# Cross-attention with layer norm on one core: the rounded copy of x moves from ScalarE to GpSimd, from the third 512 rows on

## What is computed

```python
qh = split_heads(q @ Wq.T + bq)            # q = x, (4, 2048, 512)
kh = split_heads(k @ Wk.T + bk)            # k = v = ctx, (4, 77, 512)
vh = split_heads(v @ Wv.T + bv)
scores = einsum('bhqd,bhkd->bhqk', qh, kh) / sqrt(32)
scores = where(mask == 0, -1e9, scores)
e = exp(scores - max(scores)) * mask
probs = e / (sum(e) + 1e-9)
attn = einsum('bhqk,bhkd->bhqd', probs, vh)
x = attn @ Wo.T + bo + residual            # residual = q
out = (x - mean(x)) / sqrt(var(x) + 1e-5) * ln_g + ln_b
```

## Time and profile before

| what | us |
| --- | --- |
| three runs, median | 617.98 |
| three runs, lowest to highest | 617.49 to 618.96 |
| the profiled execution, its device time | 615.88 |
| the profiled execution, its span | 614.1 |

### The profile page before, as it was taken

The page is one execution under the profiler, slowest core; times in us unless marked ns, Lnnn a source line. Parts: engine busy times, 40 slices in busy tenths (PEclk is TensorE's granted clock), DMA queues, the critical chain, the costliest instruction groups (busy, mean ns, idle before and its releaser), DMA issues.

```text
span 614.1 us, 15264 instructions
## 1 busy us (share of the span) xinstructions
PE 564.5 (92%) x5460; PEld 456.9 (74%) x5460; DVE 525.6 (86%) x801; ACT 504.6 (82%) x2288; POOL 437.5 (71%) x399
## 2 busy tenths in 40 slices
PE   2699398999999999999999999999999999999795
PEld 2588376777878788777877788777878788776574
DVE  4577558789998979898998989898998899899877
ACT  4449669899898989998898989998898999889521
POOL 2704443867588795789778886689678967786787
PEclk9989789999999999999999999999999999999899
DMA  8922730120045310640324412340424312202132
GB/s 310 318 88 57 225 88 1 52 99 3 11 140 188 138 53 10 216 147 3 94 93 155 155 64 75 122 148 3 126 76 141 153 51 104 105 2 99 76 138 102
DMA packets 36198, 64.91 MB, mean 106 GB/s; under 512 B 12443, under 2 KB 14491, under 8 KB 34075
## 3 DMA queue, kind: packets, MB, share of 16 engines
q1 hardware_dynamic: 35979, 63.94, 30.6%
q10 hardware_dynamic: 144, 0.00, 0.0%
HBM read 44.15 MB, written 19.46 MB: 104 GB/s over the span
## 4 chain that ended last, share of the span: by engine, by line
PE 84%; DVE 6%; SPq 5%; DMA 3%; issue 2%; POOL 0%; ACT 0%; DVEq 0%
PE qo_bank L420 54%; PE s_bank L420 17%; PE av_bank L508 11%; DVE E L803 2%; DMA Kd<-TP 2%; PE av_bank L420 1%; DMA Vp<-V_scratch 1%; DVE TP L832 1%; SPq L251 1%; SPq L330 1%; SPq L256 1%; DVE qo_bank L849 1%; DVE bn L855 1%; SPq L304 0%; DVE AT_lo L841 0%
## 5 line engine op out<-in xcount | busy, mean ns | idle before, releaser
L625 ACT ACTIVATE E<-E,neg_max 128x77 f32<-128x77 f32 x1024 | 352.2, 352 | 19.7 <-DVE neg_max L811 19.6
L625 ACT ACTIVATION_READ_ACCUMULATOR E<-E,neg_max 128x1 f32 x1024 | 196.8, 192 | 0.0
L1125 POOL TENSOR_TENSOR E<-E,inv_sum 128x1232 f32<-128x1232 f32 x64 | 145.7, 2279 | 66.6 <-DVE inv_sum L818 66.6
L803 DVE TENSOR_TENSOR E<-s_bank,mask_bias 128x616 f32<-128x616 f32 x128 | 101.3, 791 | 40.7 <-PE s_bank L420 38.9
L420 PE MATMUL s_bank<-Kd,QT_hi 128*128 128x308 f32 x512 | 111.7, 305 | 0.0
L832 DVE STREAM_TRANSPOSE TP<-E 128x1280 f32<-128x1280 f32 x64 | 96.1, 1502 | 4.1 <-PE av_bank L508 3.6
L811 DVE TENSOR_REDUCE neg_max<-E 128x8 f32<-128x624 f32 x128 | 98.5, 781 | 0.4
L420 PE MATMUL s_bank<-Kd,QT_lo 128*128 128x308 f32 x256 | 81.3, 317 | 15.5 <-DVE E L803 11.7
L420 PEld LDWEIGHTS s_bank<-Kd,QT_hi 128*128 128x128 f32 x512 | 84.4, 188 | 4.2
L1143 POOL TENSOR_TENSOR Y<-Y,b_row 128x512 f32<-128x512 f32 x62 | 79.2, 1297 | 4.5 <-ACT Y L642 4.2
L1105 POOL TENSOR_TENSOR xT_lo<-xT_raw,xT_hi 128x1024 fp32r<-128x1024 f32 x30 | 71.7, 2410 | 14.0 <-ACT xT_hi L602 14.0
(11 more groups left out here) (60 smaller groups left out, 790.9 us busy)
## 6 DMA issues: line engine op xcount, KB each, us to landing
Y<-in_x SPq DMA_DIRECT2D x16, 1024.0 KB, 6.1
out_y<-Y SPq DMA_DIRECT2D x64, 256.0 KB, 2.0
xT_raw<-in_xT SPq DMA_DIRECT2D x15, 1024.0 KB, 4.9
Vp<-V_scratch SPq DMA_DIRECT2D x32, 96.0 KB, 2.4
K_scratch<-TP SPq DMA_DIRECT2D x1, 1232.0 KB, 6.8
Y<-in_WqT SPq DMA_DIRECT2D x4, 256.0 KB, 8.4
xT_raw<-in_xT SPq DMA_DIRECT2D x2, 512.0 KB, 6.9
TP<-in_WvT SPq DMA_DIRECT2D x4, 256.0 KB, 7.9
```

The lines of the kernel that those rows point to most:

```text
L625: last = cp(e, e, ACT.Exp, bias=neg_max[:, t, h:h + 1], accum_out=rowsum[:, t, h:h + 1])
L803: tt(E[:, t, :, 0:SK].rearrange("p (g j) k -> p g j k", g=2), s_bank[:, :, 0:GK].rearrange("p g (j k) -> p g j k", j=HG), mask_bias[:, row ...
L1125: nc.gpsimd.tensor_tensor(out=e, in0=e, in1=inv.unsqueeze(2).broadcast_to((P, 2 * HH, SK)), op=ALU.mult).then_inc(probs_ready, 1)
```

## The change

`XT_copy` is new: it does on GpSimd what `XT_hi` did on ScalarE. Blocks 0 and 1 stay as they were; for blocks 2 to 15 (28 halves) the copy stands right ahead of the subtraction of the same half, and the 28 `XT_hi` calls are gone from ScalarE's list. Its first half waits for the load of x, as the copy on ScalarE did. The subtraction waits for a new semaphore, `x_copied`, that GpSimd raises itself. No other call changes its place on any engine. A diff of ScalarE's list of calls at one step, of GpSimd's at one step, and the functions:

```diff
@@ scalar, odd steps
-                    LN_scale(s - 5, 0), XT_hi(s - 1, 0), XT_hi(s - 1, 1), Q_hi(s - 2, 3), exponent(s - 3, 6)
-                    exponent(s - 3, 7), exponent(s - 2, 0), exponent(s - 2, 1), XT_hi(s, 0)
+                    LN_scale(s - 5, 0), Q_hi(s - 2, 3), exponent(s - 3, 6)
+                    exponent(s - 3, 7), exponent(s - 2, 0), exponent(s - 2, 1)
...
@@ gpsimd
+            def XT_copy(b, i):
+                if not has(b):
+                    return
+                if i == 0:
+                    pool.wait_ge(x_loaded[b % 2], 16 * (b // 2 + 2 - b % 2))
+                cs = slice(2 * i, 2 * i + 2)
+                nc.gpsimd.tensor_copy(xT_hi[:, b % 2, cs, :], xT_raw[:, b % 2, cs, :]).then_inc(x_copied, 1)
+
             def XT_lo(b, i):
                 if not has(b) or b == 0:
                     return
-                pool.wait_ge(xt_hi, 2 * b + i + 1)
+                if b == 1:
+                    pool.wait_ge(xt_hi, 2 * b + i + 1)
+                else:
+                    pool.wait_ge(x_copied, 2 * (b - 2) + i + 1)
...
@@ gpsimd, s == 10
-                    XT_lo(10, 0), XT_lo(10, 1), add_beta(6, 0), add_eps(8, 3), normalise(8, 3), add_bo(7, 0)
-                    add_eps(9, 0), inv_std(6, 2), normalise(9, 0), XT_lo(11, 0), XT_lo(11, 1)
+                    XT_copy(10, 0), XT_lo(10, 0), XT_copy(10, 1), XT_lo(10, 1), add_beta(6, 0), add_eps(8, 3), normalise(8, 3), add_bo(7, 0)
+                    add_eps(9, 0), inv_std(6, 2), normalise(9, 0), XT_copy(11, 0), XT_lo(11, 0), XT_copy(11, 1), XT_lo(11, 1)
...
@@ gpsimd, s == 14
-                    XT_lo(14, 0), XT_lo(14, 1), add_beta(10, 0), add_eps(12, 3), normalise(12, 3)
-                    add_bo(11, 0), inv_std(10, 2), add_eps(13, 0), XT_lo(15, 0), XT_lo(15, 1)
+                    XT_copy(14, 0), XT_lo(14, 0), XT_copy(14, 1), XT_lo(14, 1), add_beta(10, 0), add_eps(12, 3), normalise(12, 3)
+                    add_bo(11, 0), inv_std(10, 2), add_eps(13, 0), XT_copy(15, 0), XT_lo(15, 0), XT_copy(15, 1), XT_lo(15, 1)
                     normalise(13, 0), add_beta(10, 1), add_eps(13, 1), inv_std(10, 3), normalise(13, 1)
```

More of the change, by code:

```diff
@@ L705, in _ @@
                     exponent(12, 3), Q_hi(13, 1), exponent(12, 4), exponent(12, 5), Q_hi(13, 2)
[L706 to L707 removed]
+                    AT_hi_(11, 3), LN_scale(10, 0), Q_hi(13, 3), exponent(12, 6)
+                    exponent(12, 7), exponent(13, 0), exponent(13, 1),
                     Q_hi(14, 0), LN_scale(10, 1), exponent(13, 2), exponent(13, 3)
@@ L1154, in _ @@
                 elif s == 2:
-                    XT_lo(2, 0), XT_lo(2, 1), add_eps(1, 0), normalise(1, 0), XT_lo(3, 0), XT_lo(3, 1)
+                    XT_copy(2, 0), XT_lo(2, 0), XT_copy(2, 1), XT_lo(2, 1), add_eps(1, 0), normalise(1, 0), XT_copy(3, 0), XT_lo(3, 0), XT_copy(3, 1), XT_lo(3, 1)
                     add_eps(1, 1), normalise(1, 1), add_eps(1, 2), normalise(1, 2), add_eps(1, 3)
@@ L1161, in _ @@
                 elif s == 4:
-                    normalise(2, 1), normalise(2, 2), XT_lo(4, 0), XT_lo(4, 1), add_eps(2, 3)
-                    normalise(2, 3), add_eps(3, 0), inv_std(0, 0), normalise(3, 0), XT_lo(5, 0), XT_lo(5, 1)
+                    normalise(2, 1), normalise(2, 2), XT_copy(4, 0), XT_lo(4, 0), XT_copy(4, 1), XT_lo(4, 1), add_eps(2, 3)
+                    normalise(2, 3), add_eps(3, 0), inv_std(0, 0), normalise(3, 0), XT_copy(5, 0), XT_lo(5, 0), XT_copy(5, 1), XT_lo(5, 1)
                     add_eps(3, 1), inv_std(0, 1), inv_std(0, 2), inv_std(0, 3), inv_std(1, 0)
@@ L1172, in _ @@
                 elif s == 8:
-                    XT_lo(8, 0), XT_lo(8, 1), add_beta(4, 0), add_eps(6, 3), normalise(6, 3), add_bo(5, 0)
-                    add_eps(7, 0), inv_std(4, 2), normalise(7, 0), XT_lo(9, 0), XT_lo(9, 1), add_beta(4, 1)
+                    XT_copy(8, 0), XT_lo(8, 0), XT_copy(8, 1), XT_lo(8, 1), add_beta(4, 0), add_eps(6, 3), normalise(6, 3), add_bo(5, 0)
+                    add_eps(7, 0), inv_std(4, 2), normalise(7, 0), XT_copy(9, 0), XT_lo(9, 0), XT_copy(9, 1), XT_lo(9, 1), add_beta(4, 1)
                     inv_std(4, 3), add_eps(7, 1), add_beta(4, 2), add_beta(4, 3), normalise(7, 1)
@@ L1194, in _ @@
                 elif s == 12:
-                    XT_lo(12, 0), XT_lo(12, 1), add_beta(8, 0), add_eps(10, 3), normalise(10, 3)
+                    XT_copy(12, 0), XT_lo(12, 0), XT_copy(12, 1), XT_lo(12, 1), add_beta(8, 0), add_eps(10, 3), normalise(10, 3)
                     add_bo(9, 0), add_eps(11, 0), inv_std(8, 2), normalise(11, 0), add_beta(8, 1)
-                    XT_lo(13, 0), XT_lo(13, 1), inv_std(8, 3), add_eps(11, 1), add_beta(8, 2)
+                    XT_copy(13, 0), XT_lo(13, 0), XT_copy(13, 1), XT_lo(13, 1), inv_std(8, 3), add_eps(11, 1), add_beta(8, 2)
                     add_beta(8, 3), normalise(11, 1), add_bo(9, 1), add_eps(11, 2), normalise(11, 2)
```

29 lines of the change are left out of this document (15 added, 14 removed).

## The result

The changed kernel takes **621.68 us** (median of five runs, 619.13 to 622.72), the kernel before 617.98 beside it (617.14 to 618.96). The ratio is 1.0053, with a 95% interval of 1.0029 to 1.0078, that is, 1.8 to 4.8 us more. 621.4 was forecast, in a range of 618.9 to 624.8. The profiled execution took 620.44 us, 4.56 more than that of before, where 619.3 was forecast. The total is as forecast, and so, within 0.1 us, is the lateness at each place that was costed; what the three repeating pairs lose is not. One execution of a later kernel (e6) took 932.87 us at a granted clock of 0.56 in place of 0.98, and stands in none of the ranges.

The account below looks back on a forecast made before the run. PE was taken to bound the kernel. Added PE waits of 1.16 (block 3), 0.1 (4, 6), 1.11 (8, 10, 12) and 1.0 (14, 15) made 3.4 us on 617.98: 621.4 us, range 618.9 to 624.8.

Parts of the forecast that it names:

- PE is the bound, and ACT's relief is worth nothing: PE busy 67.62 of each pair's 68.60 us; taking 29.4 us of copies off ACT was costed at nothing gained.
- The copy's price: A 128x1024 copy on GpSimd: 1043 ns, plus 0.09 us wait, 1.13 us; 2.26 us for a block's two.
- Contention with DVE: Rival: GpSimd copies held up by DVE through shared ports, each block 0.9 us longer, 627.7 us; chance 0.05.
- The early casts: Four start-up GpSimd casts averaging 870 ns instead of 610, put down to VectorE's splitting of weights holding them up.
- Block 3: PE's Q(2, 2) needs the subtractions; 1.10 us slack against a block 2.26 later, so PE waits 1.16 us.
- Blocks 4 and 6: add_eps behind the split had waited 1.55 and 2.63 us for ACT; little lateness left, 0.1 us taken.
- Blocks 14 and 15: PE late 0.57 us at Q(14, 0) through center and 0.42 at Q(14, 2) through normalise, together 1.0.
- The odd blocks 5 to 13 cost nothing: Their splits stand behind a normalise with longer slack, 5.6 us at block 11 against 2.26 plus carry-over: nothing.
- Blocks 8, 10 and 12: inverse behind add_eps 0.86 us late, making center late for PE's Q(10, 0): 0.37 each, 1.11 in all.
- the second chain: Rival: late inv_std delays LN_scale, exponentials and Q_hi at blocks 9, 11, 13, 15: +2, 623.4 us; chance 0.11.
- The sum: PE's added waits at six or seven places: 1.16 + 0.1 + 1.11 + 1.0 = 3.4 us.
- "hidden" rival: Copies fit between the split and inverse's turn if each takes under 0.95 us: +1.1, 619.1 us; chance 0.20.

Follow-up runs that it names:

- e6: Changed kernel with GpSimd's list reordered around the tight places (add_eps, normalise and inv_std ahead of add_beta, also blocks 3 and 15), all 28 copies kept: 618.02 us, ratio 1.0006.
- e2: Changed kernel with the 28 copies left out altogether, products reading the rounded x of blocks 0 and 1 again: 617.75 us, ratio 1.0001.
- e1: Kernel before with ACT's copies kept and GpSimd making the same 28 once more ahead of its subtractions: 621.75 us, ratio 1.0072.
- e4: Changed kernel with only the copies of blocks 5, 7, 9, 11 and 13 on GpSimd, the others back on ACT: 616.5 us, ratio 0.9996.
- e5: Changed kernel with only the copies of even blocks 2 to 14 on GpSimd, the others back on ACT: 619.6 us, ratio 1.0032.
- e7: Changed kernel with inv_std moved ahead of add_beta on GpSimd behind the splits of blocks 9, 11, 13 and 15: 620.71 us, ratio 1.0051.

## Why the prediction was right in its total and where it was wrong

- *PE is the bound, and ACT's relief is worth nothing*: right. e2's pair is 68.61 without any copies, e1's the changed kernel's with all of them.
- *The copy's price*, 1043 ns plus 0.09: right, 1041 ns and 1.12 from start to start (the forecast's 1.13). The difference of two shapes of a relative on the same engine, taken from the half-size cast, gave it within 2 ns. Contention with DVE did not come: the 28 copies lie at 1.03 to 1.07 us. Beside this stands the rule of the Trainium skill's "SBUF — State Buffer", section "SBUF: two separate sides", an exclusive lock between GpSimd and an instruction of VectorE that is in a 2-port mode or, against a GpSimd instruction that reads SBUF, has two SBUF inputs. The trace agrees for the second condition, since in the pairs every two-input instruction on large tiles that VectorE has takes one of the two from PSUM (`s_bank`, `qo_bank`, `av_bank`).
- *The early casts*: the prediction's account of the four fits less well. In the timeline of the kernel before, only the first ran beside the splitting of weights (from 23.45, while VectorE's split lasted to 24.06). The second was the slowest, 1.18 us, and ran beside VectorE's mask instruction, which has one SBUF input; whether that was in a 2-port mode no trace here shows. The last two were as fast as the others, some 0.6 us.
- *Block 3*, 1.16: right in kind and near in size, 1.23 of lateness, and 0.08 of restart that was not in it. *Blocks 4 and 6*, 0.1: nothing. *Blocks 14 and 15*, 0.57 and 0.42: 0.51 and 0.46, the second with the first's restart in it. The transpose at block 15 was said to be 2.38 late and is 2.29 (22.73 us behind the pair's start against 20.44), of which DVE stands 1.60 for `normalise`.
- *The odd blocks 5 to 13 cost nothing*: this is the step that failed. Taken alone they are free, as e4 shows (ratio 0.9996). But each stands behind an even block, and what the two leave together, 3.03 us, is more than the 2.3 that `inv_std` could be late. I checked `Q(10, 2)` and `xt_lo`, with 5.6 us of slack, and did not follow `LN_scale`, `Q_hi` and `Q_lo` to PE; I only gave that chain a chance of 0.11.
- *Blocks 8, 10 and 12*, three times 0.37, 1.11 in all: the start of `Q(10, 0)` came 0.37 later as said (0.44 and 0.39 at the two others), but the term was not right. It took `center` as due for PE's product, 0.49 behind its end; it is due for the weight load, 0.36 behind it, and the hand-over takes 0.06 of that. `center` was 0.80 late and not 0.86, so the load is 0.50 late, and the place costs 0.48. The pairs are 2.20 longer. 0.48 each would have been the first place with its restart (e5, e7), and with the second chain it is 0.70 to 0.77. The rival was right as a mechanism, near in size (+1.1 where +2 was said), and wrong in that its cost was to be added to the first place's: "Behind that DVE meets a wait for PE's next scores, so the rest of its lateness is gone" is true of DVE, but GpSimd's lateness runs on.
- *The sum*: 3.4 said, 4.6 in the trace, 3.7 between the medians, 1.8 to 4.8 by the ratio's interval. The runs can't tell 3.4 from 4.6; the traces can. That the total of 621.4 came within 0.3 us of the median, with the second chain and every restart missing from the sum, is luck.
- The "hidden" rival (619.1) asked for a copy with its wait under 0.95; it was 1.12. In another way it came true: with the same copies and another order (e6) the loss is gone within 0.0006 [−0.0012, +0.0025].

No kernel here is faster than the one before: PE has no wait left that these edits touch, and e6, e4 and e2 all end at its time.
